# Chunk 1's normalised rows turned on TensorE instead of by DMA transposes, with waits and short work of steps 0 to 2 reordered

## The reference

```python
h = nan_to_num(take(embed_table, ids))              # 16384 rows of 256
x = layernorm(h)
f, i, c = sigmoid(x @ Wf.T), sigmoid(x @ Wi.T), g(x @ Wh.T)   # g(z) = z + 0.5 if z >= 0, else sigmoid(z)
s[t] = f[t] * s[t-1] + i[t] * c[t],  s[-1] = 0.5    # along each sequence
h = h + s
y = layernorm(h)
a = bitlinear(y, w_fc) + gate * (y @ v.T @ fast_b.T @ u.T)
h = h + bitlinear(relu(a) ** 2, w_proj)
```

## Time and profile before

| | before |
|---|---|
| median of 3 runs | 922.15 us (920.87 to 922.21) |
| the profiled execution's own time | 922.77 us |
| its span | 920.9 us |
| TensorE busy | 880.4 us, 96% of the span |
| ScalarE busy | 786.5 us, 85% |
| VectorE busy | 759.3 us, 82% |
| GpSimd busy | 416.1 us, 45% |
| granted TensorE clock, mean | 0.994 |

### The profile page before, as it was taken

How to read it: one execution, slowest core, us unless ns; L and a number is a source line. 1 busy time by engine, 2 the same in 40 slices (tenths; PEclk the granted TensorE clock), 3 DMA queues, 4 the chain that set the end, 5 groups by cost and what they waited for, 6 DMA issues and landing times.

```text
span 920.9 us, 18355 instructions
## 1 busy us (share of the span) xinstructions
PE 880.4 (96%) x5497; PEld 482.4 (52%) x5497; DVE 759.3 (82%) x1343; ACT 786.5 (85%) x1188; POOL 416.1 (45%) x457
## 2 busy tenths in 40 slices
PE   2869899999999999999999999999999999999997
PEld 1334455555545555554555555455555545555554
DVE  6769988888888888888888888888888888888766
ACT  4559888899888889988888998888899888899884
POOL 6543544554544455443445544344554444433110
PEclk9989999999999999999999999999999999999999
DMA  4212454233344323334432333443233344324311
GB/s 144 46 27 55 91 97 88 62 88 79 76 95 97 84 63 88 81 73 97 97 77 68 88 81 73 97 96 78 67 90 81 72 97 96 75 68 84 79 46 47
DMA packets 227484, 73.41 MB, mean 80 GB/s; under 512 B 202246, under 2 KB 222288, under 8 KB 227456
## 3 DMA queue, kind: packets, MB, share of 16 engines
q1 hardware_dynamic: 221312, 68.86, 33.7%
q0 software_dynamic: 6144, 4.21, 2.1%
HBM read 27.68 MB, written 24.64 MB: 57 GB/s over the span
## 4 chain that ended last, share of the span: by engine, by line
PE 87%; ACT 4%; DVE 3%; issue 2%; DMA 2%; SPq 2%; POOL 1%; ACTq 0%; DVEq 0%; POOLq 0%
PE bank L836 34%; PE bank L858 22%; PE y_ps L772 22%; PE bank L872 3%; PE turned L812 1%; PE turned L749 1%; SPq L331 1%; ACT normed L501 1%; ACT sq L575 1%; ACT relu L562 1%; PE turned L760 1%; PE turned L759 1%; DMA x_cols<-x_rows 1%; DMA spill<-hid_blocks 0%; DMA w_raw<-wh 0%
## 5 line engine op out<-in xcount | busy, mean ns | idle before, releaser
L858 PE MATMUL bank<-x_cols,fc_t 128*128 128x512 f16 x1024 | 245.1, 382 | 3.9 <-ACT relu L562 3.9
L414 POOL TENSOR_SCALAR var_eps<-moments 128x4 f32<-128x4 f32 x64 | 59.7, 932 | 397.4 <-DVE moments L1000 397.3
L836 PE MATMUL bank<-x_cols,w_hi 128*128 128x512 f16 x768 | 230.2, 382 | 7.1 <-ACT cand_lin L551 3.0
L836 PE MATMUL bank<-x_cols,w_lo 128*128 128x512 f16 x768 | 229.7, 381 | 0.0
L772 PE MATMUL y_ps<-proj_t,sq_hi 128*128 128x256 bf16 x1024 | 225.6, 273 | 3.0 <-DVE sq_lo L1179 3.0
L772 PE MATMUL y_ps<-proj_t,sq_lo 128*128 128x256 bf16 x1024 | 225.6, 273 | 0.0
L562 ACT ACTIVATE relu<-bank,relu_scale 128x512 f32<-128x512 f32 x256 | 159.3, 689 | 39.9 <-PE bank L872 39.0
L404 POOL DMA_INDIRECT rows_raw<-table,idx_now x128 | 143.2, 1119 | 59.9 <-issue 30.8
L858 PEld LDWEIGHTS bank<-x_cols,fc_t 128*128 128x128 bf16 x1024 | 95.3, 98 | 131.6 <-issue 29.2
L1179 DVE TENSOR_TENSOR sq_lo<-sq,sq_hi 128x1024 f16<-128x1024 f32 x128 | 150.6, 1214 | 5.8 <-ACT sq L575 5.7
L501 ACT ACTIVATE normed<-h,shift,rstd 128x256 f32<-128x256 f32 x256 | 132.6, 601 | 6.4 <-POOL shift L422 6.3
(11 more groups left out here) (143 smaller groups left out, 918.6 us busy)
## 6 DMA issues: line engine op xcount, KB each, us to landing
out<-out_sb SPq DMA_DIRECT2D x31, 512.0 KB, 3.0
spill<-hid_blocks SPq DMA_DIRECT2D x30, 256.0 KB, 2.1
hid_rows<-spill SPq DMA_DIRECT2D x120, 64.0 KB
rows_raw<-table,idx_now POOLq DMA_INDIRECT x128, 2.6
x_cols<-x_rows SPq DMA_TRANSPOSE x122, 3.3
sq<-w_fc SPq DMA_DIRECT2D x1, 1024.0 KB, 6.6
pj_raw<-w_proj SPq DMA_DIRECT2D x1, 1024.0 KB, 4.8
out<-out_sb SPq DMA_DIRECT2D x2, 256.0 KB, 2.2
```

The costliest lines, as they stand in the source:

```text
L836: ins = pe.matmul(gate_bank(p, par)[:, :], w[:, k, q, :], x_part(0, par, part)[:, :, k, :], start=(k == 0 and w is w_hi and part == 0), st ...
L858: ins = pe.matmul(fc_bank(f, par)[:, :], fc_t[:, f, k, :], x_part(1, 0, part)[:, :, k, :], start=(opens and k == 0 and part == 0), stop=(n ...
```

## The change

It has five parts.

1. Chunk 1 of k = 0 goes the way of chunk 0: TensorE turns its rows between gates 3 and 4 of step 0, ACT and DVE split them from `turned`. `x_high(0, 1)`, `x_low(0, 1)` and the two DMA transposes go. `by_dma` counts the semaphores accordingly, one less for k = 0.
2. In step 0 gates 4 and 5 wait for 1 and 2 evictions (before: 4 and 4), in step 1 gates 0 to 3 for 4, 5, 6 and 8 evictions of step 0 (before: 8 each). These are the evictions of the bank that each writes.
3. POOL issues chunk 1's fourth gather behind `root(0, 0)` instead of ahead of it.
4. In step 1 `turn_bound` moves ahead of `turn_hidden(0)`, `spread_proj_scale` to the end of TensorE's list, and the wait for `u_landed` to the first `narrow`. `set_output_scales` is split: `set_relu_scale` goes to DVE's step 0, `set_proj_scale` behind the ternary `w_proj` of step 1.
5. Order on DVE and ACT: `make_ternary` of `w_fc` moves behind the scans of step 0; `measure_next` of step 1 ahead of `cols_low(1)`; the candidate of step 1 ahead of `halve_scales`; on ACT `scale_fc(1)` ahead of one eviction, `part_high(0)` behind two; in step 2 `x_high(0, 3)` and `x_low(0, 3)` come earlier.

```diff
+        def by_dma(k, c):
+            return c if k else c - 1
...
             def turn_rows(k, c, par):
-                    sp.wait_ge(ready, c)
+                    sp.wait_ge(ready, by_dma(k, c))
...
                 if isinstance(n, int) and n == 0:
-                    turn_rows(0, 1, 1)
                     turn_fc(0)
...
-            gather(1, 1)
+            gather(1, 1, range(TILES - 1))
             root(0, 0)
+            gather(1, 1, (TILES - 1,))
...
                     normalise(0, 1, h0[:, 1, :, :])
-                    x_high(0, 1)
                     evict(0, par, 0, 2, cand_sig, ACT.Sigmoid)
                     evict(0, par, 0, 3, cand_lin, ACT.Identity, 0.5)
                     evict(0, par, 1, 0, forget, ACT.Sigmoid)
+                    cols_high(0, 1)
...
                     evict(1, par, 1, 0, forget, ACT.Sigmoid)
+                    scale_fc(1)
                     evict(1, par, 1, 1, inp, ACT.Sigmoid)
                     normalise(1, 0, h1[:, 0, :, :])
                     cols_high(1)
-                    scale_fc(1)
-                    part_high(0)
                     evict(1, par, 1, 2, cand_sig, ACT.Sigmoid)
                     evict(1, par, 1, 3, cand_lin, ACT.Identity, 0.5)
+                    part_high(0)
...
                     normalise(0, 3, h0[:, 1, :, :])
+                    x_high(0, 3)
                     part_high(1)
-                    x_high(0, 3)
...
                         if first:
-                            pe.wait_ge(gate_taken, 8)
+                            pe.wait_ge(gate_taken, (4, 5, 6, 8)[p])
                     else:
-                        pe.wait_ge(gate_taken, 8 * n + (4, 4 if start else 3)[p - 4])
+                        pe.wait_ge(gate_taken, 8 * n + ((1, 2) if start else (4, 3))[p - 4])
...
+                    elif first:
+                        pe.wait_ge(cols_lo[0], 4)
                     else:
-                        pe.wait_ge(x_landed[0], 32 * n)
+                        pe.wait_ge(x_landed[0], 32 * (n - 1))
                     for p in range(3):
                         gate(p)
                     if first:
+                        turn_bound()
                         turn_hidden(0)
...
                     gate(3)
+                    if start:
+                        turn_normed(0, 1)
                     gate(4)
...
-                if first:
-                    turn_bound()
-                    spread_proj_scale()
-                    pe.wait_ge(u_landed, 16)
                 wide(0, True)
                 wide(1, True)
...
                     wide(3, True)
+                    if first:
+                        pe.wait_ge(u_landed, 16)
                     narrow(0, 4)
...
                 wide(7, False)
+                if first:
+                    spread_proj_scale()
...
                 if start:
-                    make_ternary(fc_raw, fc_a, fc_s, fc_b, range(4), fc_ready)
-                    x_low(0, 1)
                     candidate(0)
                     weigh(0)
+                    cols_low(0, 1)
                     scan(0)
+                    make_ternary(fc_raw, fc_a, fc_s, fc_b, range(4), fc_ready)
                     candidate(1)
                     weigh(1)
                     scan(1)
+                    make_ternary(fc_raw, fc_a, fc_s, fc_b, range(4, FC), fc_ready)
                     residual(0, 0)
                     split_u()
+                    set_relu_scale()
                     guard(2, 64, 0)
                     guard_sum(2, 0)
-                    make_ternary(fc_raw, fc_a, fc_s, fc_b, range(4, FC), fc_ready)
                     return
                 if first:
+                    measure_next()
                     cols_low(1)
-                    measure_next()
                     part_low()
+                    candidate(0)
+                    weigh(0)
+                    low_low()
+                    scan(0)
                     halve_scales(pj_s, FC + KD, HID)
                     spread_scales()
-                    low_low()
-                    candidate(0)
-                    weigh(0)
-                    set_output_scales()
-                    scan(0)
                     x_low(0, 2)
...
                     make_ternary(pj_raw, pj_a, pj_s, pj_c, range(KD), pj_ready)
+                    set_proj_scale()
                     residual(1, 1)
...
+                if second:
+                    x_low(0, 3)
                 scale_output(n - 2)
                 part_low()
-                if ahead:
+                if ahead and not second:
                     x_low(0, n + 1)
```

More of the change, by code:

```diff
@@ L495, in normalise @@
                 act.wait_ge(rstd_ready[k], c + 1)
-                if isinstance(c, int) and c == 1:
-                    act.wait_ge(cols_turned[k], TILES)
-                wait(act, x_hi_ready[k], c - 1)
-                wait(act, x_lo_ready[k], c - 1)
+                if isinstance(c, int) and c > 0 and by_dma(k, c - 1) <= 0:
+                    act.wait_ge(cols_turned[k], TILES * c)
+                wait(act, x_hi_ready[k], by_dma(k, c - 1))
+                wait(act, x_lo_ready[k], by_dma(k, c - 1))
                 for j in range(TILES):
@@ L506, in x_high @@
                 act.wait_ge(normed_ready[k], TILES * (c + 1))
-                wait(act, x_landed[k], 32 * (c - 1))
+                wait(act, x_landed[k], 32 * by_dma(k, c - 1))
                 act.activation(x_rows[k][:, 0, :, :], normed[k][:, :, :], ACT.Copy).then_inc(x_hi_ready[k], 1)
             def cols_high(k, again=0):
-                if again:
+                if again and k:
                     act.wait_ge(fc_done, FC * (N - 1))
@@ L515, in cols_high @@
                     act.wait_ge(cols_turned[k], TILES * again + 2 * q + 2)
-                    act.activation(x_part(k, 0, 0)[:, 2 * q:2 * q + 2, :, :], turned_cols(q), ACT.Copy)\
+                    act.activation(x_part(k, 0 if k else again, 0)[:, 2 * q:2 * q + 2, :, :], turned_cols(q), ACT.Copy)\
                         .then_inc(cols_hi[k], 1)
@@ L712, in turn_normed @@
             def turn_normed(k, c=0):
-                wait(pe, h1_ready, c + 1 if c else 0)
+                wait(pe, h1_ready, c + 1 if c and k else 0)
                 for j in range(TILES):
@@ L1002, in x_low @@
             def x_low(k, c):
-                dve.wait_ge(x_hi_ready[k], c)
+                dve.wait_ge(x_hi_ready[k], by_dma(k, c))
                 dve.tensor_tensor(x_rows[k][:, 1, :, :], normed[k][:, :, :], x_rows[k][:, 0, :, :], ALU.subtract)\
@@ L1008, in cols_low @@
             def cols_low(k, again=0):
-                if again:
+                if again and k:
                     dve.wait_ge(fc_done, FC * (N - 1))
+                par = 0 if k else again
                 for q in range(2):
                     dve.wait_ge(cols_hi[k], 2 * again + q + 1)
-                    dve.tensor_tensor(x_part(k, 0, 1)[:, 2 * q:2 * q + 2, :, :], turned_cols(q),
-                                      x_part(k, 0, 0)[:, 2 * q:2 * q + 2, :, :], ALU.subtract).then_inc(cols_lo[k], 1)
+                    dve.tensor_tensor(x_part(k, par, 1)[:, 2 * q:2 * q + 2, :, :], turned_cols(q),
+                                      x_part(k, par, 0)[:, 2 * q:2 * q + 2, :, :], ALU.subtract).then_inc(cols_lo[k], 1)
             def scale_low_rank():
@@ L1108, in split_u, with set_relu_scale @@
                     .then_inc(u_split, 1)
-            def set_output_scales():
+            def set_relu_scale():
                 dve.wait_ge(bound_spread, 1)
-                dve.wait_ge(pj_spread, 1)
                 mark(dve.tensor_reduce(bound_2[:, :], y_ps[:, 2, P:D], AX, ALU.max))
@@ L1124, in set_output_scales, with set_proj_scale @@
                 mark(dve.tensor_tensor(grow[:, :], grow[:, :], grow[:, :], ALU.mult))
+            def set_proj_scale():
                 settle()
+                dve.wait_ge(pj_spread, 1)
                 dve.tensor_scalar(proj_scale[:, :], y_ps[:, 3, :], grow[:, :], None, ALU.mult).then_inc(u_ready, 1)
@@ L1216, in step @@
                 first = isinstance(n, int) and n == 1
+                second = isinstance(n, int) and n == 2
                 ahead = known_below(n, N - 1)
```

## The result

| | before | changed |
|---|---|---|
| median, measured side by side (4 runs each) | 922.18 us (920.87 to 924.12) | 916.34 us (915.88 to 916.36) |
| ratio, 95% interval | | 0.9933 [0.9921, 0.9945] |
| profiled execution, its span | 922.77, 920.9 us | 916.36, 914.5 us |
| TensorE busy | 880.4 us | 879.4 us |

What follows compares the result with a forecast made beforehand. TensorE is busy throughout the later steps, so only reaching step 3 earlier saves time. Terms -1.2 - 2.2 + 0.3 - 3.6 + 0.2 + 0.25 = -6.25 us take 922.15 to 915.9 us; range 913.4 to 919.4.

Steps and rivals of the forecast that it cites:

- A: Step 0, chunk 1's fourth gather behind the root: root, first `normed` and first gate come earlier, -1.2 us.
- B: Steps 0 to 1, chunk 1 turned on TensorE and gates waiting only for own banks: residual starts earlier, -2.2 us.
- C: Step 1, DVE's work before the second norm's columns, now with `set_relu_scale` and chunk 2's statistics: +0.3 us.
- D: Step 1, TensorE's wait for the spread `w_proj` scales ahead of the first wide block goes: -3.6 us.
- E: Step 1, clock at half, back 3 us after `low_parts`: eight wide matmuls take 2.95 us, +0.2 (bounds -1.0 to +1.1).
- F: Step 1 to 2: clip gains 0.2, scale spread ahead of step 2's gates costs 0.45; +0.25 us, between -0.4 and +0.8.
- G: Step 2, `x_low(0, 3)` ahead of `part_low(1)`: hidden by TensorE's wait for chunk 3's columns; 0, at worst +0.7 us.
- Rival 1: GpSimd's small instructions held up at their new places, at both roots: +1.2 us on average, 917.1 us; chance 0.14.
- Rival 2: DMA chain for chunk 3's columns does not move, TensorE waits at 107.10 as before: time stays 922; chance 0.04.
- Rival 3: Half clock does not come back from first wide block to step 2's gate 2: +3.0 us, 925.2 us; chance 0.03.

Runs made afterwards that it cites:

- second trace of the changed kernel: The changed kernel run once more with no edit, beside the kernel before on another chip: ratio 0.9952 [0.9931, 0.9973].
- kernel before with D alone: The kernel before with only the spread of `w_proj`'s scales moved to the end of TensorE's step 1 and DVE's scales split: ratio 0.9932, 927.23 us for 933.67.

## Why the prediction came out as it did

Forecast 915.9, measured 916.34: the saving was 5.84 of 6.25 us. The steps below are from one trace of each kernel; the second trace of the changed kernel has its starts 1.0 to 1.5 us earlier.

- **A** was right in place: -1.17 at the first `normed`, -1.01 at gate 0 of step 0. The range of this term was the clock's, and so was part of its scatter: `turn_hidden(0)` lay between 41.61 and 43.68 in the kernels with the same step 0.
- **B** was right in place and size: A and B together gave -3.74 at `turn_hidden(0)` for -3.4. The 0.3 us more are luck of this trace: the matmuls reached full rate 4.1 us behind gate 0 and not 5.0. The two runs that undo its halves show more than the forecast said, namely that the banks earn only with the turn beside them.
- **C** was right: from -3.74 at `turn_hidden(0)` to -3.46 at `cols_low(1)` (52.91 for 56.37), +0.28 for +0.3.
- **D** was right: -3.66 between `low_parts` and the first wide block for -3.6, shown from both sides.
- **E** was mis-sized. The eight wide matmuls took 0.63 us more than before (3.39 for 2.76 between starts), not 0.2, and the two `low_sums` behind them 0.34: nearly all of them ran at half rate. The term is +0.97. The step that failed is "with the clock back 3 us after `low_parts`". TensorE resumed at 54.22 and the full clock came just ahead of 59, 4.6 us later; in the second trace of the same kernel the eight took 3.02. Taking one moment from the earlier trace rows as fixed was wrong; the bound, eight and `low_sums` at half rate, +1.1, held.
- **F** had its sign wrong. The clip gained 0.29 more, as said, and the spread took its place ahead of step 2's gate 0 (0.61 us with the tail). But the stretch at half rate that the kernel before had there (70.9 to 74.3) is gone, which I had as the favourable bound: from the clip to gate 0 of step 2 the shift grew by 1.04 us, and ACT's eviction kept 0.57 of it. The term is -0.86 for +0.25.
- **G** was right up to step 4 and failed behind it. The part "0" looked only at step 3's gate. With `x_low(0, 3)` early, `part_low(1)` is late by 0.56 us, and so are the clips of step 2, which come 5.68 us behind `low_parts` instead of 4.97. ACT makes this good in step 3: its `part_hi` there stands 28.14 us behind `low_parts` of step 2, 28.10 in the kernel with `x_low(0, 3)` put back. But TensorE waits 0.77 us at gate 0 of step 5 (154.51) for its columns. The chain that ends there:

```profile
133.17 1.96 ACT normed L505 x4
135.15 1.07 ACT x_rows L512
136.24 1.23 DVE x_rows L1014
...
140.90 2.88 DMA spill<-hid_blocks
...
148.18 1.78 SPq L302
...
150.00 4.38 DMA x_cols<-x_rows
...
154.51 5.35 PE bank L840 x24
```

Up to the issue of the transposes it is nearly level, 60.30 us behind `low_parts` of step 2 and 60.10 with `x_low(0, 3)` put back. The late part is the transposes themselves. From issue to landing (median, around gate 0 of step 5), the changed kernel, then the kernel before:

```profile
x_cols<-x_rows SPq DMA_TRANSPOSE x4, 4.9
x_cols<-x_rows SPq DMA_TRANSPOSE x4, 3.5
```

With `x_low(0, 3)` put back it is 3.5 too. Between 152 and 153 us, in the midst of them, the changed kernel's DMAs moved only 5 GB/s. All ten traces with 27.50 us or more from step 4 to step 5 have such a gap and, some 3.0 to 3.7 us behind the issue of these transposes, a packet of the queue that the profile calls instruction. The other four, with 27.10 us or less, have no gap, and that packet comes more than 4.2 us behind the issue. One of the four has the early `x_low(0, 3)`: the kernel with chunk 1 by DMA. So the late clips are not the cause, and the early `x_low(0, 3)` does not bring the loss by itself. That the packet holds the transposes up would fit all fourteen, but was not tried; the cause stays open.

**Rival 1**, GpSimd held up at its new places, did not hold. The second norm's `shift` took 0.20 us where it had taken 0.93, and the first root was not late (17.66 for a forecast of about 17.5). The other side was held up instead, off the path:

```profile
21.34 0.97 POOL L394 MEMSET rows_raw<- 128x1024 f32 x1
```

```profile
20.49 1.85 DVE L1047 COPY low_a<-a_hi 128x32 f16<-128x32 f16 x1
```

The copy took 0.17 us before; now it started beside the moved gather (20.18 to 21.33) and ended at 22.34, with the end of GpSimd's memset behind it. The price at gate 0 was 0.2 us at most: from `normed` to it 4.39 us for 4.23. The Trainium skill, "SBUF — State Buffer", section "Who interferes with whom", says that a DVE copy can contend with GpSimd for a shared pair of ports, that whoever issues first has the pair for its whole instruction, and that the order of issue decides who waits. The row agrees in that the copy was held up by GpSimd, the side that rival 1 left out; that it waited for the memset too, which started 0.85 us behind it, goes beyond what the section says.

**Rival 2** did not occur: TensorE's wait for chunk 3's columns shrank from 1.57 to 0.65 us. The 0.7 to 0.9 us of step 5 were lost to DMAs as well, but by another way and two steps later than I looked.

**Rival 3** did not occur: the clock came back.

The terms that were off (A and B -0.3, E +0.8, F -1.1, G +0.7 behind step 4) nearly cancel. The total was nearer than its parts, and that is luck.

## What to carry to other kernels

A wait can hide another: own banks alone moved nothing while the DMA transposes were late, and 1.8 us with them gone. So price an edit with its neighbour in place before calling it small. An edit that is free at the next meeting point is to be followed further: here 0.7 us were lost two steps on, and the lateness that the edit had caused was not the reason. And idle time on TensorE just ahead of dense work can cost more than its own length: behind the waits of 2.0 and 2.6 us shown above the matmuls ran at half rate.

## What the hardware showed beside this

In the first two groups of runs, on two chips, ScalarE began `part_hi` up to 1.7 us after TensorE's `low_parts` had released it, in many of the steady steps, with a releaser that the profile calls remote:

```profile
252.00 0.60 ACT L537 ACTIVATE part_hi<-turned 128x512 f16<-128x512 f32 x1 [2.19 <-remote]
```

TensorE then waited for `part_lo`. Between 110 and 850 us, in the second trace of the changed kernel:

```profile
PE turned L763 <- DVE part_lo L1296: 12.8, 10, 1.4
```

In the first trace of the same kernel that group is missing. Ten waits of 1.3 us are the 12.8 us that this execution was longer. The kernel before with D alone had five such waits (6.8 us), so they occur without the rest of the change. The kernel before itself was not traced on these two chips. In the first group its median was only 1.4 us above that of the result, while the changed kernel with the gather ahead of the root, 4.8 us ahead of it by step 5, was level with it in the whole time (ratio 0.9996). Whether the change makes the waits more frequent stays open, as does what on the chip causes them, which was not tried.

The moment at which TensorE's matmuls first start 0.22 and not 0.43 us apart moved between 26.7 and 30.5 us among the kernels. In the first trace of the changed kernel the granted clock stands at 0.50 up to it; in other traces, that of the kernel before among them, it reads 1.00 over the same stretch of half rate, so there the spacing is the surer sign. With the first gates at half rate up to it, this alone moves step 1 by about a microsecond, as much as part A is worth. And the clock followed idle time in both directions when TensorE was kept at work: a fall avoided at one place came at the next wait.
